# A pre-norm transformer block: the attention loop rewritten as one pipeline whose stages lie a step apart

## The reference

```
h    = layernorm(x)
q,k,v = h@wq, h@wk, h@wv            # 16 heads of 128
q,k  = rotary(q), rotary(k)         # x*cos + swapped halves(x)*sin
attn = softmax(q k^T / sqrt(128)), key in (query-128, query]
x    = x + (attn v) @ wo
g    = gelu(layernorm(x) @ ternary(w1) + b1)
out  = x + g @ ternary(w2) + b2
```

## Time and profile before

| what | us |
|---|---|
| median of 3 runs (394.19 to 397.13) | 395.04 |
| the profiled execution | 393.5 |
| its span, first to last instruction | 391.4 |
| PE busy | 358.2 |
| DVE busy | 353.3 |
| ACT, POOL busy | 241.1, 243.8 |
| TensorE's mean granted clock | 0.983 |

### The profile page before, as it was taken

One profiled execution on the slowest core, in us unless ns is written; L12 is line 12 of the kernel. 1 busy time (PEld: TensorE's weight loads), 2 busy tenths in 40 slices (PEclk: granted clock), 3 DMA queues, 4 the chain that ended last, 5 costly groups with the idle time before them and its releaser, 6 DMA issues.

```text
span 391.4 us, 7121 instructions
## 1 busy us (share of the span) xinstructions
PE 358.2 (92%) x2418; PEld 322.0 (82%) x2418; DVE 353.3 (90%) x660; ACT 241.1 (62%) x686; POOL 243.8 (62%) x186
## 2 busy tenths in 40 slices
PE   6977899999999999999999999999999988859697
PEld 5866788888888888889888988889888887757597
DVE  5978889999899989999999999989999999999971
ACT  2547878766776667666766676667667656417510
POOL 2336666666666666658665866666666548746970
PEclk9998999999999999999999999999999999969989
DMA  7863533233423342334233423342223220000002
GB/s 222 253 211 90 139 79 98 54 84 81 110 54 82 80 109 57 80 82 107 55 81 83 107 55 82 80 108 57 55 54 67 70 55 1 2 0 0 2 27 82
DMA packets 28147, 31.27 MB, mean 80 GB/s; under 512 B 3280, under 2 KB 19152, under 8 KB 28112
## 3 DMA queue, kind: packets, MB, share of 16 engines
q1 hardware_dynamic: 28112, 30.82, 30.2%
HBM read 12.98 MB, written 1.05 MB: 36 GB/s over the span
## 4 chain that ended last, share of the span: by engine, by line
DVE 48%; PE 21%; issue 13%; ACT 12%; POOL 2%; DMA 2%; SPq 1%; DVEq 0%; POOLq 0%
DVE gT_lo L784 10%; DVE probsT L818 6%; DVE rowmax L804 5%; ACT probs L600 5%; DVE turn L757 5%; PE VO L428 4%; PE PR L351 4%; DVE SC L801 4%; PE OT L409 4%; DVE negmax L806 3%; ACT gT_hi L610 3%; PE SC L387 3%; DVE SC L798 2%; DVE gT_lo L824 2%; ACT probs L592 2%
## 5 line engine op out<-in xcount | busy, mean ns | idle before, releaser
L1024 POOL TENSOR_TENSOR turn<-turn,swapped 128x512 f32<-128x512 f32 x60 | 78.0, 1300 | 81.9 <-DVE turn L757 81.8
L1021 POOL TENSOR_TENSOR swapped<-swapped,sin_sb 128x512 f32<-128x512 f32 x60 | 80.8, 1347 | 30.3 <-DMA swapped<-turn 29.6
L409 PE MATMUL OT<-probsT,v_sb 128*128 128x128 f32 x480 | 66.1, 279 | 5.4 <-DVE probsT L818 5.3
L592 ACT ACTIVATE probs<-SC,negmax 128x128 f32<-128x128 f32 x128 | 45.9, 363 | 36.4 <-DVE negmax L806 36.4
L409 PEld LDWEIGHTS OT<-probsT,v_sb 128*128 128x128 f32 x480 | 58.9, 191 | 10.1 <-DVE probsT L818 10.1
L784 DVE TENSOR_TENSOR gT_lo<-turn,gT_hi 128x512 fp32r<-128x512 f32 x62 | 65.9, 1063 | 0.3 <-ACT gT_hi L586 0.2
L600 ACT ACTIVATE probs<-probs,rinv 128x128 f32<-128x128 f32 x128 | 44.5, 395 | 28.4 <-DVE rinv L811 28.3
L586 ACT CAST gT_hi<-turn 128x512 fp32r<-128x512 f32 x64 | 39.7, 620 | 33.1 <-POOL turn L1024 29.8
L351 PE MATMUL PR<-xT_hi,qk_lo 128*128 128x512 f32 x128 | 56.1, 438 | 0.2 <-DVE mean_abs L835 0.2
L757 DVE TENSOR_TENSOR turn<-turn,cos_sb 128x512 f32<-128x512 f32 x61 | 49.9, 818 | 1.4 <-DMA swapped<-turn 1.3
L351 PE MATMUL PR<-xT_hi,qk_hi 128*128 128x512 f32 x128 | 51.0, 399 | 0.0
(11 more groups left out here) (115 smaller groups left out, 926.4 us busy)
## 6 DMA issues: line engine op xcount, KB each, us to landing
swapped<-turn SPq DMA_DIRECT2D x128, 128.0 KB, 2.3
qk_raw<-in_wq SPq DMA_DIRECT2D x16, 128.0 KB, 2.5
qk_raw<-in_wk SPq DMA_DIRECT2D x16, 128.0 KB, 2.3
v_raw<-in_wv SPq DMA_DIRECT2D x8, 256.0 KB, 2.9
o_raw<-in_wo SPq DMA_DIRECT2D x8, 256.0 KB, 4.0
xres<-in_x SPq DMA_DIRECT2D x4, 256.0 KB, 3.3
w_raw<-in_w1t SPq DMA_DIRECT2D x1, 1024.0 KB, 5.0
w_raw<-in_w2t SPq DMA_DIRECT2D x2, 512.0 KB, 3.6
```

Source lines behind the costliest of these rows:

```text
L409: last = mm(OT[:, i * P:(i + 1) * P], v_sb[:, t - 1 + b, a * HD:(a + 1) * HD], probsT[:, i, b], start=(b == b0), stop=(b == 1))
L592: nc.scalar.activation(probs[j % 2][:, i], SC[j % 2][:, i * 256 + P:(i + 1) * 256], ACT.Exp, bias=negmax[:, j % 2, i:i + 1], scale=SCALE, ...
L1021: tt(swapped[c][:], swapped[c][:], sin_sb[:, half_of(c)], ALU.mult).then_inc(sin_done, 1)
L1024: tt(turn[c][:], turn[c][:], swapped[c][:], ALU.add).then_inc(rot_done, 1)
```

## The change

All loops are written out again. What differs:

- **Rotation.** `copy_proj` is gone. DVE multiplies the projection twice, straight from `PR`: `times_sin` into `by_sin`, `times_cos` into `turn`. The swap DMA takes `by_sin` (the sin table is loaded with its halves exchanged), POOL adds, ACT casts, POOL subtracts (`rotlo` moved from DVE). Every second product carries the scale too, which leaves `exps` and `merge`: the reduction negates by itself and L806 goes.
- **Order.** In step n every engine does: PE scores(n), project(n+4), transpose_probs(n-1), a fill, weigh_v(n-1); DVE ot_lo(n-2), merge(n), mask_pt(n-1), times_sin(n+4), inverse_sum(n), times_cos(n+4), add_out of the fill of n-1; ACT ot_hi(n-2), exps(n), copy_v, scale_probs(n), rothi(n+3); POOL rotlo(n+2), rotate(n+3). The fill is given by `fills`: steps 3 to 6 of the first pair have none; the last eight steps interleave the two last heads and have v, v, v, o, oo, oo, o, none. `project_out` has two sets of `o_hi`, `o_lo` and runs two steps later than before.
- **Ternary weights** are made in the loop, from step 25 on, in eight pieces on POOL (`below`) and DVE (`ternary`); their means of absolute values come at step 20.
- **Tail.** Gelu stays in PSUM (banks PR and SC), ACT and DVE take turns with the cast, DVE does every subtraction. The first half's second product and the second half's layer norm lie before the second half's first product. The two last `project_out` lie behind the loop.

```diff
-            def project(head, a, c, m, split=None):
...
+            def project(m, split=None):
+                head, c = chunk(m)
...
+                if m >= 2:
+                    pe.wait_ge(cos_done, m - 1)
...
-                        last = mm(PR[c % 2][:], wt[:, c % 2, kd], xt[:, kd, half_of(c)],
+                        last = mm(PR[m % 2][:], wt[:, c % 2, kd], xt[:, kd, half_of(c)],
...
+            def project_out(w):
+                p, c = w // 4, w % 4
+                if c == 0:
+                    pe.wait_ge(olo_done, p + 1)
+                pe.wait_ge(otlo_done, max(step_of[2 * p, c], step_of[2 * p + 1, c]) + 1)
+                bank_free("o", w)
...
+            def scores(n):
+                head, j = step(n)
+                if j % 2 == 0:
+                    pe.wait_ge(rotlo_done, chunk_of[head, j + 1] + 1)
+                if n >= 2:
                     pe.wait_ge(exp_done, 2 * n - 2)
...
-            def pair_steps(pair, first, last):
-                for s in range(LAST_STEPS if last else 8):
-                    n = 8 * pair + s
-                    a, j = s // 4, s % 4
...
-                        pe.wait_ge(mean_read, 2)
-                    project(2 * pair + a + 1, 1 - a, j, n + 4)
...
-                    if first and s == 0:
-                        project_v(0, 2, 2)
...
-                    if s % 2 == 1:
-                        scores(n + 1, 2 * pair + (s + 1) // 4, (s + 1) // 4 % 2, (s + 1) % 4)
+            def fill(n):
+                for kind, i in fills(n):
+                    (project_v if kind == "v" else project_out)(i)
+            def ffn1(k):
+                half, f = k // NF, k % NF
+                if k == 0:
+                    pe.wait_ge(tern_done, 4)
+                if k in (2, 3):
+                    pe.wait_ge(exp_done, 2 * STEPS)
+                if k >= 4:
+                    pe.wait_ge(glo_done, k - 3)
...
-            pair_steps(PAIRS - 1, False, True)
-            transpose_probs(LAST - 4, 3)
-            project_out(PAIRS - 2, 3, 4 * PAIRS - 5)
...
-            scores(LAST - 1, 2 * PAIRS - 1, 1, 2)
-            weigh_v(LAST - 3, PAIRS - 1, 1, 0)
-            transpose_probs(LAST - 2, 1)
-            scores(LAST, 2 * PAIRS - 1, 1, 3)
...
+            project_v(0)
+            project(2, KD)
+            project(3)
+            for n in range(STEPS):
+                scores(n)
+                if n + 4 < CHUNKS:
+                    project(n + 4)
+                if n == MEANS_AT:
+                    means_of_abs()
+                if n > 0:
+                    transpose_probs(n - 1)
+                fill(n)
+                if n > 0:
+                    weigh_v(n - 1)
+            project_out(4 * PAIRS - 2)
+            transpose_probs(STEPS - 1)
             transpose_x(1, 0)
-            project_out(PAIRS - 1, 3, 4 * PAIRS - 1)
...
+            weigh_v(STEPS - 1)
+            ffn1(0)
+            ffn1(1)
+            project_out(4 * PAIRS - 1)
+            for k in range(2, NF):
+                ffn1(k)
+            ffn2(0)
+            transpose_x(1, 1)
+            ffn2(1)
+            for k in range(NF, 2 * NF):
+                ffn1(k)
+            ffn2(2)
+            ffn2(3)
```

ACT, and then DVE and POOL:

```diff
-            def copy_proj(c, m):
-                act.wait_ge(proj_done, m + 1)
-                if not (isinstance(m, int) and m < 4):
-                    act.wait_ge(rotlo_done, m - 3)
-                copy(turn[c][:], PR[c % 2][:]).then_inc(proj_copied, 1)
...
-                    nc.scalar.activation(probs[j % 2][:, i], SC[j % 2][:, i * 256 + P:(i + 1) * 256], ACT.Exp,
-                                         bias=negmax[:, j % 2, i:i + 1], scale=SCALE,
-                                         accum_out=rowsum[:, j % 2, i:i + 1]).then_inc(exp_done, 1)
...
+                    nc.scalar.activation(probs[n % 2][:, i], SC[n % 2][:, i * 256 + P:(i + 1) * 256], ACT.Exp,
+                                         bias=negmax[:, n % 2, i:i + 1],
+                                         accum_out=rowsum[:, n % 2, i:i + 1]).then_inc(exp_done, 1)
...
+            def gelu(k):
+                act.wait_ge(h_done, k + 1)
+                nc.scalar.activation(hb[k % 4][:], hb[k % 4][:], ACT.Gelu,
+                                     bias=b1_sb[:, k % NF:k % NF + 1]).then_inc(gelu_done, 1)
...
+            for n in range(STEPS):
+                p, s = n // 8, n % 8
+                if n >= 2:
+                    ot_hi(n - 2)
+                exps(n)
+                if n > 0:
+                    for kind, i in fills(n - 1):
+                        if kind == "v":
+                            copy_v(i)
+                scale_probs(n)
+                if n + 3 < CHUNKS:
+                    rothi(n + 3)
+                if s == 1 and p < PAIRS - 1:
...
+            def times_table(dest, m, table):
+                c = chunk(m)[1]
+                if c % 2 == 0:
+                    return nc.vector.scalar_tensor_tensor(dest[:], PR[m % 2][:], SCALE, table[:, half_of(c)],
+                                                          ALU.mult, ALU.mult)
+                return tt(dest[:], PR[m % 2][:], table[:, half_of(c)], ALU.mult)
+            def times_sin(m):
+                dve.wait_ge(proj_done, m + 1)
+                if m >= 2:
+                    dve.wait_ge(rot_done, m - 1)
+                times_table(by_sin[m % 2], m, sin_sb).then_inc(sin_done, 1)
+            def times_cos(m):
+                if m >= 4:
+                    dve.wait_ge(rotlo_done, m - 3)
+                times_table(turn[m % 4], m, cos_sb).then_inc(cos_done, 1)
...
-                    nc.vector.copy_predicated(sc[:, 0, 1], in_prev_sb[:], nothing[:])
+                    tt(sc[:, 0, 1], sc[:, 0, 1], no_prev[:], ALU.add)
...
-                nc.vector.tensor_reduce(rowmax[:, j % 2], sc[:, :, 1], AX.X, ALU.max).then_inc(max_done, 1)
-                dve.wait_ge(max_done, n + 1)
-                nc.vector.tensor_scalar(negmax[:, j % 2], rowmax[:, j % 2], -SCALE, None,
-                                        ALU.mult).then_inc(negmax_done, 1)
-            def inverse_sum(n, j):
+                nc.vector.tensor_reduce(negmax[:, n % 2], sc[:, :, 1], AX.X, ALU.max,
+                                        negate=True).then_inc(negmax_done, 1)
...
+            for n in range(STEPS):
+                if n >= 2:
+                    ot_lo(n - 2)
+                merge(n)
+                if n == STEPS - 1:
+                    add_out(4 * PAIRS - 3)
+                    tile_stats(1, 2)
+                    tile_stats(1, 3)
+                    moments(1, 0)
+                if n > 0:
+                    mask_pt(n - 1)
+                if n == MEANS_AT:
+                    thresholds()
+                if n + 4 < CHUNKS:
+                    times_sin(n + 4)
+                inverse_sum(n)
+                if n + 4 < CHUNKS:
+                    times_cos(n + 4)
+                if 0 < n < STEPS - 1:
+                    for kind, w in fills(n - 1):
+                        if kind == "o":
+                            add_out(w)
...
+                i = (n - BELOW_AT - 1) // 2
+                if n > BELOW_AT and (n - BELOW_AT) % 2 == 1 and i < PIECES:
+                    ternary(i)
```

POOL, whose function `rotate` and loop are shown:

```diff
-                tt(swapped[c][:], swapped[c][:], sin_sb[:, half_of(c)], ALU.mult).then_inc(sin_done, 1)
...
+            def rotate(m):
+                pool.wait_ge(swap_in[m % 2], 32 * (m // 2 + 1))
                 pool.wait_ge(cos_done, m + 1)
...
+            for n in range(STEPS - 2):
+                p, s = n // 8, n % 8
+                rotlo(n + 2)
+                if n + 3 < CHUNKS:
+                    rotate(n + 3)
```

More of the change, by code:

```diff
@@ L941, in _ @@
[L941 to L951 removed]
+            nc.vector.copy_predicated(no_prev[:], in_prev_sb[:], nothing[:]).then_inc(no_prev_set, 1)
+            times_sin(3)
+            times_cos(3)
@@ L997, in _ @@
+            xt_lo(1, 1)
+            for t in range(4):
+                finish(t)
+            for k in range(NF, 2 * NF, 2):
+                ghi(k)
+                glo(k)
+                glo(k + 1)
+            for t in range(4, NT):
+                finish(t)
         @block.gpsimd
```

915 lines of the change are left out of this document (350 added, 565 removed).

## The result

The changed kernel takes 382.73 us in the median (380.63 to 384.32, 4 runs), the kernel before 395.81 beside it (394.19 to 397.13, 4 runs): a ratio of 0.967, 95% interval 0.961 to 0.973. Forecast were 375 us and a range of 367 to 387. So the direction and the range held, and 7.7 us of the gain did not come. The profiled run took 382.7 us, with a span of 380.9 and a clock of 0.978.

A forecast was written before the change was run, and what follows sets the result against it. DVE was taken to bound the old loop, PE the new one. Span 22.4 + 36.0 + 226.0 + 38.7 + 48.4 = 371.5, +2.1 makes 373.6, and 1.5 more for the median gives 375 us; range 367 to 387.

The forecast's parts named there:

- DVE is the bound of the loop, PE 0.3 behind it.: Old loop: DVE's instructions sum to 4.96 us against a step of 4.95; PE needs 4.63.
- The step, 4.67: New loop, steps 8 to 55: PE's 4.63 plus a few hundredths; 48 x 4.67 + 1.8 = 226.0 us, minus 11.8.
- DVE's prices: New loop: products from PSUM taken as 0.68 and 0.72 us, giving DVE a step of 3.84.
- near 85%: Sign in the profile: DVE's busy share between scores(8) and scores(56).
- Well under PE's 4.63.: New loop: even with both products at 0.76 us, DVE's step is 3.96, below PE's.
- The first rival: Loop stays at 4.95 us a step through handing over, `mask_pt`'s slack only 0.45: +11.8, 387 us; chance 0.15.
- `abs_sums` and `ternary`, 1.8: Steps 10 to 17 and 26 to 40: these lengthen ACT and DVE, adding 1.8 us.
- Steps 56 to 63, 38.7: Last eight steps: 31.9 us plus bank waits of 1.2, 2.8 and 2.8 in steps 60 to 62; 38.7, plus 7.1.
- Start and steps 0 to 7: First scores at 22.4 us, plus 1.0; steps 0 to 7 take 9.0 + 4.7 + 17.6 + 4.7 = 36.0, minus 5.4.
- Tail, 48.4: From the end of scores(63) to the end of the span: 48.4 us, minus 10.8.
- PE no longer idle: Sign in the tail: PE no longer idles 5 us before x is transposed.
- The slower rival: Rotation's swap chain delays scores; a step over 5.35 us makes the whole slower; at 5.5, 415 us; chance 0.05.

The follow-up runs named there:

- two matmuls fewer: Low-part product of q and k weights left out of every projection: kernel before 390.59 us (395.45 beside it), changed kernel 375.06 us.
- the multiplication: Changed kernel with the row maximum's sign turned by a separate DVE multiplication again, instead of by the reduction: 408.33 us, ratio to before 1.032.
- the run with the remainder late: Changed kernel with the low part of the rotated chunk computed on DVE instead of POOL, at the end of DVE's step: 404.02 us.
- the run with them in even steps: Changed kernel with the sums of absolute values in even steps 10 to 24 instead of steps 10 to 17, mean and thresholds 6 steps later: 382.27 us.
- the run that kept PE busy: Changed kernel with ten small constant products added on PE before each of three bank waits in steps 60 to 62: 381.13 us.
- the run with the comparison put later: Kernel before with the sign turned by the reduction and POOL's w2 comparison waiting until DVE normalised the second norm's first half: 372.83 us.
- the repairs: Changed kernel with head 15's weights earlier, additions ahead of merges in steps 60 to 63, absolute sums in even steps, thresholds 8 steps later: 368.44 us.

## Why the prediction was right, and where not

- **"DVE is the bound of the loop, PE 0.3 behind it."** Half shown. PE isn't: two matmuls fewer gave 3.0 us in the old loop. For DVE, the 4.96 is a sum of mean durations, three of which (L806, L784, L757) hold times of waiting for GpSimd; by the earlier trace rows DVE was busy 4.68 a step. Load and ring were not told apart. In the new loop PE has no idle time in quiet pairs.
- **The step, 4.67.** Measured 4.55: 48 x 0.12 = 5.8 us better. The few hundredths added to PE's 4.63 for the new order weren't there.
- **DVE's prices.** The products from PSUM took 0.67 to 0.68, also in the three-operand form for which I took 0.72. DVE's work in steps 8 to 55 is 3.54 us a step against 3.84, and its busy share there 74%, where the sign said near 85%. The Trainium skill ("VectorE: DVE Perf Modes", Rules for kernel authors) leaves two ways open, a matmul's result at the slowest mode, or a copy first. The trace speaks for the first: the direct products took 0.69 us at most, and L757 from SBUF had 818 ns in the mean, 662 at least and 1732 at most.
- **"Well under PE's 4.63."** Wrong as a reason, and the deepest error, since the sum didn't show it: a load of 3.84 on DVE was taken as room. The prediction worked out DVE's order up to the next `merge`, "just level", but never closed the ring through mask, weighting, `ot_hi` and `ot_lo`. The first rival had named the mask's slack of 0.45 as the weak place, and that is where it broke. ACT's casts, the thresholds, the multiplication and the remainder each lengthened steps while DVE stayed far from full: busy 199.78 of 243.3 us in the run with the remainder late.
- **`abs_sums` and `ternary`, 1.8.** Mis-sized. Steps 8 to 23 alone lost 3.1 us to the sums, by the run with them in even steps. `ternary` cost nothing that shows: steps 24 to 31 took 4.55 us each.
- **Step 54.** No term of the sum had it: 5.8 us. The order of the last pair's chunks was read for the fills, but not for the first need of head 15's weights.
- **Steps 56 to 63, 38.7.** The bank waits were 7.0 us as forecast (6.8). The stage took 42.2, since the clock fell behind two of them, 3.1 us by the run that kept PE busy.
- **Start and steps 0 to 7.** +1.0 and +1.3. scores(2) came 9.0 us after scores(0), as worked out, and steps 3 to 6 took 17.7 (17.6). Step 2 took 6.0 instead of 4.7: PE waited 1.12 for the mask.
- **Tail, 48.4.** Measured 49.4. `normalise` took 1.38, taken as 1.7; the run with the comparison put later shows that this overlap was worth 5 us by itself. PE still idled 3.3 us ahead of the weighting and 1.1 ahead of fill 30, which then took 2.7 us instead of 1.44, at a clock of 0.50. So the sign "PE no longer idle" came only in part.
- **The slower rival.** Its bound has a wrong sum: from 375 us, a step of 5.09, and not of 5.35, makes the whole slower than 395. It didn't come: the swap landed in 2.3 us, and in steps 8 to 55 PE never waited for the remainder before its scores.
- **What makes the gain.** The text counted L806's 0.64 as the smallest of three reliefs of DVE. By itself it is the whole gain in the loop and more; as they were made, the other edits cost 4 us beside it. With the repairs the new order is 4.4 us ahead of the old one with its comparison put later (368.4 to 372.8).

Sum of the misses in span: 1.0 + 1.3 + 2.6 + 3.5 + 1.0 = 9.4, which is 380.9 - 371.5. The 2.6 of steps 8 to 55 is 5.8 for step 54, less 5.8 for the shorter step, and a rest of 2.6 beyond the 1.8, put down to sums and thresholds. That the two 5.8 cancel is luck; so is a part of the hit, since most of the gain came from an instruction to which the prediction gave the least weight.

Why the old order bears the multiplication better than the new one stays open; no run took its queues apart. One thing the traces show: when L806 goes from the old order, L757 gets longer by 0.35 us in the mean, while the new order's DVE step, outside the steps with thresholds and `ternary`, holds no other instruction that was lengthened.

## What to carry over

A two-column instruction with a mean of 0.64 us is a question, not a price: try the edit that removes it alone before rewriting the order around it. In a pipeline over several engines, write the shortest ring of waits that returns to itself, with what each queue puts ahead of its links, beside the load of each engine; an engine 74% busy has no room if its instructions stand in that ring. And where the order of work changes at the end of a loop, look for the first use of everything that is prepared by step number.
